# Graph layer and experts on one core: the sources' one-hots built by one wide comparison on VectorE and one wide product on GpSimd

## The reference

```python
deg = segment_sum(ones, dst); dinv = where(deg > 0, deg ** -0.5, 0)
norm = dinv[src] * dinv[dst]
for l in range(5):
    edge_fea = concat([edge_attr[:, 3:] @ ew1[l], edge_attr[:, 0:3] @ ew2[l]])
    agg = segment_sum(norm[:, None] * (h[src] + edge_fea), dst)
    h = relu(concat([h, agg]) @ mlp_w[l] + mlp_b[l]);  h = batch_norm(h);  h = relu(h)
```

## Time and profile before

| | |
|---|---|
| median of 3 runs | 1647.67 us (1642.39 to 1649.33) |
| profiled execution | 1643.12 us, span 1641.4 us |
| TensorE (PE) busy | 1429.9 us, 87% of the span |
| VectorE (DVE) busy | 706.7 us, 43% |
| ScalarE (ACT) busy | 389.4 us, 24% |
| GpSimd (POOL) busy | 173.8 us, 11% |
| the count build | from about 166 to 436 us of the span |

### The profile page before, as it was taken

How to read it: one execution, slowest core, us unless ns; L and a number is a source line. 1 busy time by engine, 2 the same in 40 slices (tenths; PEclk the granted TensorE clock), 3 DMA queues, 4 the chain that set the end, 5 groups by cost and what they waited for, 6 DMA issues and landing times.

```text
span 1641.4 us, 26069 instructions
## 1 busy us (share of the span) xinstructions
PE 1429.9 (87%) x8986; PEld 851.2 (52%) x8987; DVE 706.7 (43%) x1938; ACT 389.4 (24%) x1010; POOL 173.8 (11%) x145
## 2 busy tenths in 40 slices
PE   2565689899889999989999899998999963899996
PEld 2554444444443544535444454444545441899995
DVE  6989999999622220122101230012300176334332
ACT  1320454444401400023000320014100131244442
POOL 1000000000000000000000000000000001577774
PEclk9875789999999999999999999999999966899998
DMA  5153000000000000000000000000001464144443
GB/s 138 40 177 135 1 2 1 2 1 2 14 1 0 14 1 0 1 15 1 1 1 0 15 1 1 0 1 13 1 1 30 75 221 143 35 69 71 67 73 45
DMA packets 49553, 57.90 MB, mean 35 GB/s; under 512 B 14320, under 2 KB 41602, under 8 KB 49185
## 3 DMA queue, kind: packets, MB, share of 16 engines
q1 hardware_dynamic: 38688, 41.67, 8.9%
q0 software_dynamic: 10752, 14.69, 5.5%
HBM read 42.36 MB, written 13.99 MB: 34 GB/s over the span
## 4 chain that ended last, share of the span: by engine, by line
PE 80%; DVE 12%; issue 3%; DVEq 1%; ACT 1%; DMA 1%; POOL 1%; SPq 0%; POOLq 0%
PE bank L653 42%; PE bank L734 14%; PE bank L1152 6%; PE bank L1161 6%; PE bank L1747 3%; PE bank L1692 2%; DVE ohL L1404 1%; DVE ohS L1518 1%; PE bank L643 1%; PE bank L737 1%; PE bank L1745 1%; PE bank L1143 1%; PE bank L1118 1%; PE bank L1096 1%; DVE xst L1390 0%
## 5 line engine op out<-in xcount | busy, mean ns | idle before, releaser
L653 PE MATMUL bank<-at,m 125*128 125x500 fp8e4 (+1 forms) x3500 | 700.2, 356 | 9.5 <-issue 4.1
L653 PEld LDWEIGHTS bank<-at,m 125*128 125x128 f16 x3500 | 318.9, 98 | 343.5 <-issue 37.6
L662 DVE TENSOR_TENSOR aggT<-bank,dinvB 128x500 f32<-128x500 f32 (+1 forms) x70 | 42.3, 621 | 352.3 <-PE bank L653 352.2
L825 ACT ACTIVATE hT<-bank,prm 128x500 f32<-128x500 f32 (+1 forms) x70 | 40.5, 630 | 602.5 <-PE bank L737 602.5
L873 POOL TENSOR_TENSOR idJ<-idJ,wts 125x1400 f32<-125x1400 f32 x2 | 8.0, 4006 | 1379.9 <-DVE idJ L1031 1379.9
L787 DVE BATCH_NORM_STATS2 zst<-hT 128x6 f32<-128x500 f32 (+1 forms) x70 | 40.3, 617 | 199.7 <-ACT hT L825 199.7
L734 PE MATMUL bank<-hT,wcur 128*128 128x500 f32 (+1 forms) x280 | 125.3, 570 | 0.0
L1518 DVE TENSOR_SCALAR ohS<-iotaS,now 128x128 bf16<-128x128 bf16 x504 | 117.6, 306 | 0.0
L734 PE MATMUL bank<-aggT,wcur 128*128 128x500 f32 (+1 forms) x280 | 116.6, 539 | 0.0
L1152 PEld LDWEIGHTS bank<-xtT,w1c 128*128 128x128 f32 x896 | 109.8, 194 | 2.8
L622 DVE SCALAR_TENSOR_TENSOR m<-bank,dinvP,m 125x256 f16<-125x256 f32 x100 | 48.0, 483 | 144.7 <-ACT m L634 144.7
(11 more groups left out here) (316 smaller groups left out, 1271.3 us busy)
## 6 DMA issues: line engine op xcount, KB each, us to landing
slrow<-sl_dram SPq DMA_DIRECT2D x26, 512.0 KB, 5.0
w1s<-in_L_ffn_W SPq DMA_DIRECT2D x1, 4096.0 KB, 14.2
w2s<-in_L_ffn_W SPq DMA_DIRECT2D x1, 4096.0 KB, 19.0
xin<-in_x SPq DMA_DIRECT2D x1, 2800.0 KB
x<-in_x SPq DMA_DIRECT2D x1, 2800.0 KB
out_rows<-x SPq DMA_DIRECT2D x1, 2800.0 KB
xn_dram<-xn SPq DMA_DIRECT2D x1, 2800.0 KB
wraw<-in_L_gnn_mlp_w SPq DMA_DIRECT2D x5, 512.0 KB, 3.6
```

The source lines that it names most:

```text
L653: last = pe.matmul(bank[banks[g % len(banks)]][:, 0:w], m[:, s, k, h * 128:(h + 1) * 128], at_block(g // H)[:, s, :], start=s == 0 and k = ...
```

## The change

The index table `iotaS` and the buffers `ohS` take the layout by pairs that `ohD` and `cnt1` have. VectorE now makes the plain one-hots of all eight chunks by one comparison of 1024 elements a partition, the first of its three, and increments a new semaphore `s_one[side]`; `s_oh[side]` is incremented by the last of the other two. GpSimd gets a loop over all windows, `powers`, which waits for `s_one[side]`, multiplies `ohS` in place by the powers of row 13, and increments `s_pow[side]`. TensorE waits for `s_pow[side]` ahead of the count products, and reads `ohS` with a step of two elements. `by_pairs` is only moved.

```diff
-        iotaS = r("iotaS", [128, 128], BF16)
+        iotaS = r("iotaS", [128, 128, 2], BF16)
...
-        ohS_1 = r("ohS_1", [128, U, 128], BF16)
+        ohS_1 = r("ohS_1", [128, U // 2, 128, 2], BF16)
...
+        def powers(pool, w):
+
+            side = w % 2
+            mine, past = turns(pool, w), turns_before(pool, w)
+            with pool.Fori(0, mine) as i:
+                pool.wait_ge(s_one[side], past + i + 1)
+                pool.sem_inc(s_apart, 1)
+                pool.tensor_tensor(ohS[side][:, :, :, :], ohS[side][:, :, :, :], by_pairs(now[:, side, 13, :], 128), ALU.mult).then_inc(s_pow[side], 1)
+
+        def by_pairs(a, width):
+
+            n = a.shape[1] // 2
+            return a.rearrange("p (c k) -> p c k", k=2).unsqueeze(2).to_broadcast([128, n, width, 2])
...
-            pool.iota(iotaS[:, :], pattern=[[1, 128]], base=0, channel_multiplier=0, allow_small_or_imprecise_dtypes=True).then_inc(s_mem, 1)
+            pool.iota(iotaS[:, :, :], pattern=[[1, 128], [0, 2]], base=0, channel_multiplier=0, allow_small_or_imprecise_dtypes=True).then_inc(s_mem, 1)
...
+            pool.wait_ge(s_rng, 1)
+            for w in range(NW):
+                powers(pool, w)
             gather_pool(pool)
             experts_pool(pool, step)
...
                     dve.wait_ge(s_now[side], past + i + 1)
+                    dve.tensor_tensor(ohS[side][:, :, :, :], to_all(iotaS[:, :, :], U // 2), by_pairs(now[:, side, 12, :], 128), ALU.is_equal).then_inc(s_one[side], 1)
                     dve.tensor_tensor(ohD[side][:, :, :, :], to_all(iotaD2[:, :, :], U // 2), by_pairs(nowKD[:, side, 1, :], W), ALU.is_equal)
-                    dve.tensor_tensor(cnt1[side][:, :, :, :], to_all(iotaK[:, :, :], U // 2), by_pairs(nowKD[:, side, 0, :], GW), ALU.is_equal)
-                    for j in range(U):
-                        last = dve.tensor_scalar(ohS[side][:, j, :], iotaS[:, :], now[:, side, 12, j:j + 1], now[:, side, 13, j:j + 1], ALU.is_equal, ALU.mult)
-                    last.then_inc(s_oh[side], 1)
+                    dve.tensor_tensor(cnt1[side][:, :, :, :], to_all(iotaK[:, :, :], U // 2), by_pairs(nowKD[:, side, 0, :], GW), ALU.is_equal).then_inc(s_oh[side], 1)
...
                         pe.matmul(sums_w, now[:, side, 0:12, j], ohD[side][:, j // 2, :, j % 2], start=False, stop=False)
+                    pe.wait_ge(s_pow[side], past + i + 1)
+                    pe.sem_inc(s_apart, 1)
                     for j in range(U):
-                        last = pe.matmul(out_w, ohS[side][:, j, :], cnt1[side][:, j // 2, :, j % 2].rearrange("p (g n) -> p g n", g=GROUPS),
+                        last = pe.matmul(out_w, ohS[side][:, j // 2, :, j % 2], cnt1[side][:, j // 2, :, j % 2].rearrange("p (g n) -> p g n", g=GROUPS),
                                          start=False, stop=False)
```

More of the change, by code:

```diff
@@ L189, in gnn_ffn_program @@
         r = Region((NT * 6 * CQ + 31) // 32 * 32)
-        ohS_0 = r("ohS_0", [128, U, 128], BF16)
+        ohS_0 = r("ohS_0", [128, U // 2, 128, 2], BF16)
         ohD_0 = r("ohD_0", [128, U // 2, W, 2], BF16)
@@ L362, in gnn_ffn_program @@
         s_now = [sem(f"s_now{r}") for r in range(2)]
+        s_one = [sem(f"s_one{r}") for r in range(2)]
+        s_pow = [sem(f"s_pow{r}") for r in range(2)]
         s_oh = [sem(f"s_oh{r}") for r in range(2)]
@@ L1369, in _ @@
             dve.tensor_tensor(rng[:, 2 * LANES:3 * LANES], rngf[:, 2, :], rngf[:, 1, :], ALU.subtract).then_inc(s_rng, 1)
-            def by_pairs(a, width):
-                n = a.shape[1] // 2
-                return a.rearrange("p (c k) -> p c k", k=2).unsqueeze(2).to_broadcast([128, n, width, 2])
             def to_all(a, n):
```

## The result

The kernel after takes 1663.36 us, the median of 4 runs (1659.86 to 1666.04); the kernel before, on the same chip, takes 1646.24 us (1642.39 to 1649.33). The ratio is 1.0104, with a 95% interval of 1.0087 to 1.0121: 1% slower, 17 us, where 2% and 33 us were forecast. The profiled execution took 1663.09 us, with a span of 1661.3.

A forecast was written before the change was run, and what follows sets the result against it. VectorE's chain was taken to bound the count build, TensorE nearly tied: 63 windows +41.6 us, waits for TensorE -7.0, end lag -1.4, net +33.2 on 1643.12 gives 1676.3; 4.6 to the median makes 1681 us, range 1640 to 1750.

The forecast's parts named there:

- the turns and their size: Count build: GpSimd's product and VectorE's two-input operations run in turns, in 16 bits too; hold 1.76 us; 0.55, 1681 us.
- no exclusion in 16 bits: Count build: the product runs beside VectorE's 16-bit comparisons, TensorE sets the end; -26 us, 1622 us; chance 0.15.
- half the hold: Count build: 16-bit elements go twice as fast, the product holds VectorE 0.88 us a window; 1626 us; chance 0.05.
- slow product: GpSimd's product, reading powers in runs of two, takes 2.88 us; chain 71 us longer again, 1752 us; chance 0.17.
- who sets the end: Count build after the change: VectorE sets the end at 4.79 us a window against TensorE's 4.09.
- the lag at the end: End of count build: TensorE's last count weights start 2.6 us after the last one-hot was ready; expected 1.2, so -1.4.
- the fourth rival: TensorE also slows, by strided weights or waits keeping its clock down: 5 to 15 us more, 1686 to 1696; chance 0.08.
- the term of a window: VectorE, each of 63 windows: -1.79 scalar operations, +0.60 comparison, +1.85 hold = +0.66 us; x63 = +41.6.
- the overlap of the two VectorE operations that the product parts: VectorE, each window: 0.09 us added to the 1.76 us hold for lost overlap between two operations, giving 1.85.
- By then VectorE is in the 0.28 us comparison for `ohD`, and the 1192 ns one for `cnt1` waits behind the product: Where the hold falls in a window: the product starts during `ohD`'s comparison and holds up `cnt1`'s.
- VectorE's chain: VectorE's run from the copy at 166.4 to the last one-hot: 266.9 us before, 266.9 - 7.0 + 41.6 = 301.5 forecast.
- the faster rivals: Count build: "no exclusion in 16 bits" (1622 us) and "half the hold" (1626 us), both outside the range; together 0.2.

The follow-up runs named there:

- the first experiment: Changed kernel with GpSimd's product released by the comparison for `cnt1` instead of the one for `ohS`: 1672.04 us, ratio 1.0158.

## Why the prediction was off by half

**Right: the turns and their size.** GpSimd's product and VectorE's operations shut each other out in 16 bits as in 32. The hold was sized at 1.76 us from the earlier trace rows and measures 1.76; for the copy 1.49 instead of 0.19, for the mask 2.05 instead of 0.41. The rival "no exclusion in 16 bits" is refuted, and so is "half the hold" (0.88 was its hold for the whole product; that is what half of the elements bring, 0.86) and the "slow product" (1.89 us released by itself). The Trainium skill (SBUF — State Buffer, section "Who interferes with whom") names the operations that contend with GpSimd: VectorE's with two inputs in SBUF, and copies and scalar operations in their two-port modes. The runs agree: comparisons, copy and mask were held, the eviction with an input in PSUM was not, 0.68 us. The Trainium skill (GPSIMD Engine Reference, section 3.1) would have had 2.22 us for the product by the prediction's estimate; the measured 1.76 decides.

**Right: who sets the end, and the small terms.** TensorE has room, and the lag at the end shrinks by 1.8 us (1.4 said). VectorE's waits for TensorE, 7.0 us, went. The comparison takes 0.693 us (0.688 said). Weights with a step of two load as before, 98 ns in the median as in the earlier trace rows. TensorE's granted clock in the second stretch fell from 0.95 to 0.91, as the fourth rival had feared, but that stayed covered: the last count products begin 0.15 us behind GpSimd's last product.

**Wrong: the term of a window, +0.66 us, and with it +41.6 of the sum.** The size of the hold is right, but not its price, and two steps of the prediction failed.

The larger one is "and 0.09 for the overlap of the two VectorE operations that the product parts: 1.85". A plain window grew by 0.52 us (3.48 to 4.00) and not by 0.66. With 1.79 gone and 0.61 for the new comparison, the hold costs 1.70, less than its 1.76 and not more, because the start of the held operation (0.12 to 0.14 us) lies beneath it: the held copy ends 0.05 us after the product. The experiment with `cnt1` first shows that the place of the hold doesn't matter for this: its plain window is 4.01 too. 63 times 0.14 is 8.8 us.

The other is "By then VectorE is in the 0.28 us comparison for `ohD`, and the 1192 ns one for `cnt1` waits behind the product". It is the product that waits behind `cnt1`, so the hold falls at the window's end, where the evictions, 8 of 0.6 us, run beside it: 4.8 us, which the sum had left in VectorE's chain. The experiment with `cnt1` first lays them open again, and they cost 4.7.

The loads of the sequencer the prediction didn't know of. They were hidden before and are hidden now, so they cost the kernel after nothing (the product on GpSimd with fewer loads: no change); but without the hold's cover each plain window pays 0.3 to 0.45 us.

VectorE's chain was forecast at 301.5 us and is 286.6 (166.43 to 453.02), 14.9 less: 8.8 and 4.8 of that are named above, and 1.3 are left, in windows of before that had taken longer than their kind. The stage was forecast to end at about 471 (the sum itself gives 469), and the last count weights start at 453.8.

Why `cnt1` goes first was a close thing. The product is recorded from 0.19 us after the comparison that releases it has ended (175.44 and 175.63), where the prediction had taken 0.15; VectorE's start on `cnt1` is recorded 0.01 us behind it (175.64), and within 0.02 us in all 63 windows. Wherever else GpSimd's product met an operation of VectorE with all its operands in SBUF in the count builds of these runs, the one whose start is recorded first ran first: a product that starts 0.26 us behind `cnt1` waits for it and holds `ohD`, which starts later (the experiment with `cnt1` first); a mask that starts 0.13 us ahead of the product isn't held, and the next one is (the first experiment). Only the near tie is open: the comparison wins it each time, and no run shows why.

**Wrong: the price of the faster rivals.** "No exclusion" was put at -26 us and "half the hold" at -22 to -26. The runs nearest to them (two elements multiplied, half of them multiplied) gave -17 and -5. VectorE was taken to need 1.19 us less a window and got 0.74 (3.48 to 2.74), since the loads came into the open, and the two-deep buffers let through less than was counted, which is argued from the waits and not tested: with two elements multiplied, VectorE waited 25.8 us for buffers and 19.9 for evictions, and TensorE still 9.2 us for it after the first window.

## What to carry to other kernels

Work that moves from VectorE to GpSimd isn't off VectorE's path while both touch SBUF: this product takes 1.76 us of VectorE's time on GpSimd and 0.68 us on VectorE, so eight scalar operations (1.79 us) were replaced by a comparison and a hold as long as they were. To price such a hold, find first where it falls: let the GpSimd instruction wait for the operation of VectorE that is running when it starts, or starts within 0.02 us of it, but not for one that is merely next in line, and count the hold against what comes behind, leaving out what can run beside it (here the eviction fed from PSUM, the sequencer's loads, and the first 0.12 to 0.14 us of the held operation). Where short operations give way to a wide one, look for the sequencer's work that ran beneath them; here the wide forms were worth 0.3% with their product on VectorE, and 0.8% with one of three loads left out in six of eight windows.

## What was not expected of the hardware

- An instruction of GpSimd is recorded from its issue, its wait for VectorE included: 2 elements 1.26 us, 512 elements 2.10, 1024 elements 2.96, all with 1.19 us of comparison ahead.
- A mask with a scalar on 32-bit integers (125x500) is held as well, 2.05 us instead of 0.41, and so is a copy of 112 elements.
- Loading three numbers for a window keeps VectorE's sequencer busy for some 1.5 us (3 times 0.30, 0.18 to 0.20 and 0.02), which three or four wide instructions don't always cover.
